# Five edits around the first Mamba block and the last output, and three ways of weighing a Mamba state

## The reference, cut to what matters

```python
u = _silu(cb + sum((xpad[:, k:k + Ls, :] * cw[:, k] for k in range(DCV))))
dt = jax.nn.softplus(jnp.einsum('blr,cr->blc', dt_in, dw) + db)
def step(h, inp):
    dt_t, B_t, C_t, u_t = inp
    dA = jnp.exp(dt_t[..., None] * A)
    h = dA * h + (dt_t * u_t)[..., None] * B_t[:, None, :]
    y = jnp.einsum('bcn,bn->bc', h, C_t)
    return (h, y)
y = (ys + u * Dp) * _silu(z)
m = _layernorm(m + einsum('blc,dc->bld', y, wo), ln_g, ln_b)
```

## Time and profile before

| | us |
|---|---|
| median of 3 runs (2123.95 to 2128.16) | 2124.9 |
| the profiled execution | 2123.37 |
| its span, first to last instruction | 2121.5 |
| PE, DVE, ACT, POOL busy in it | 1841.3, 1634.3, 1323.1, 1015.5 |
| first scan of Mamba starts | 35.4 |
| last operation of the first block on DVE | 815.1 |
| mean granted TensorE clock | 0.943 of 2.4 GHz |

### The profile page before, as it was taken

The page is one execution under the profiler, slowest core; times in us unless marked ns, Lnnn a source line. Parts: engine busy times, 40 slices in busy tenths (PEclk is TensorE's granted clock), DMA queues, the critical chain, the costliest instruction groups (busy, mean ns, idle before and its releaser), DMA issues. The chain is left out here.

```text
span 2121.5 us, 49383 instructions
## 1 busy us (share of the span) xinstructions
PE 1841.3 (87%) x19527; PEld 1346.4 (63%) x19527; DVE 1634.3 (77%) x2595; ACT 1323.1 (62%) x2681; POOL 1015.5 (48%) x782
## 2 busy tenths in 40 slices
PE   8899889898888778987878787897798799999999
PEld 4444444444443335445567787676776599999999
DVE  5999999999999994768475442546544689998996
ACT  6988887778876643123544444342646488888886
POOL 3787777777777881100037777200630133333333
PEclk9999999999999998997879999898988799999999
DMA  5444444444445441600148889303720411112000
GB/s 191 128 137 140 132 145 134 136 140 133 136 140 144 133 115 41 155 9 1 28 127 270 253 264 249 86 0 116 245 65 12 191 66 66 66 66 77 7 7 7
DMA packets 98037, 241.63 MB, mean 114 GB/s; under 512 B 15024, under 2 KB 48320, under 8 KB 95504
## 3 DMA queue, kind: packets, MB, share of 16 engines
q1 hardware_dynamic: 89120, 218.12, 33.4%
q0 software_dynamic: 7680, 15.74, 3.2%
q10 hardware_dynamic: 1008, 4.62, 0.6%
HBM read 226.25 MB, written 12.19 MB: 112 GB/s over the span
## 5 line engine op out<-in xcount | busy, mean ns | idle before, releaser
L1346 POOL TENSOR_TENSOR dBu<-du,Bs 128x858 f32<-128x858 f32 (+1 forms) x240 | 589.2, 2457 | 184.4 <-DVE hst L1251 95.0
L573 PE MATMUL py<-hst,ident 128*128 128x429 f32 (+1 forms) x960 | 405.9, 551 | 78.6 <-DVE hst L1261 78.3
L1251 DVE TENSOR_TENSOR_SCAN hst<-dA,dBu 128x858 f32<-128x858 f32 (+1 forms) x240 | 458.3, 1910 | 6.6 <-ACT dA L1036 4.0
L573 PEld LDWEIGHTS py<-hst,ident 128*128 128x128 f32 x960 | 178.1, 197 | 269.3 <-DVE hst L1261 150.4
L1036 ACT ACTIVATE dA<-dt,negA 128x416 f32<-128x416 f32 (+1 forms) x480 | 269.9, 596 | 115.2 <-DVE hst L1251 113.5
L3671 POOL TENSOR_TENSOR hm<-h,mw 128x264 f32<-128x264 f32 x128 | 89.8, 701 | 390.7 <-DVE h L3651 390.7
L1261 DVE TENSOR_TENSOR hst<-hst,Cs 128x858 f32<-128x858 f32 (+1 forms) x240 | 247.3, 1030 | 0.0
L3542 PE MATMUL pg<-xm,wi 128*128 128x66 f16 x6144 | 214.3, 195 | 8.2 <-issue 6.8
L3542 PE MATMUL pg<-hs,wh 128*128 128x66 f16 x6144 | 217.5, 194 | 2.9 <-issue 2.9
L3542 PEld LDWEIGHTS pg<-xm,wi 128*128 128x128 f16 x6144 | 201.6, 98 | 12.8 <-issue 7.5
L3542 PEld LDWEIGHTS pg<-hs,wh 128*128 128x128 f16 x6144 | 203.8, 98 | 6.5 <-issue 3.1
(11 more groups left out here) (600 smaller groups left out, 3471.5 us busy)
## 6 DMA issues: line engine op xcount, KB each, us to landing
wb<-sf_w SPq DMA_DIRECT2D x96, 514.0 KB, 5.3
Bs<-bc_rows SPq DMA_DIRECT2D x96, 429.0 KB, 4.6
Cs<-bc_rows SPq DMA_DIRECT2D x96, 429.0 KB, 3.5
mw<-route_weights SPq DMA_DIRECT2D x8, 2112.0 KB, 10.0
wb<-gf_w SPq DMA_DIRECT2D x24, 514.0 KB, 4.9
Bs<-bc_rows SPq DMA_DIRECT2D x24, 396.0 KB, 5.2
Cs<-bc_rows SPq DMA_DIRECT2D x24, 396.0 KB, 4.3
mb<-route_masks SPq DMA_DIRECT2D x8, 1088.0 KB, 12.7
```

The source lines that it names most:

```text
L573: return nc.tensor.matmul(out, weight, moving, **kw)
L1251: v.tensor_tensor_scan(hst[:, g % HR, 0:2 * n], dA[:, g % 2, 0:2 * n], dBu[:, g % 2, 0:2 * n], 0.0, ALU.mult, ALU.add).then_inc(h_ready, 1)
L1346: g_.tensor_tensor(dBu[:, g % 2, 0:2 * n].rearrange("p (a n) -> p a n", a=2), du[:, j % 2, :, 0:n], Bs[:, q % NBS, k % BG, 0:n].unsqueeze( ...
```

## The change

- avg and eps are set by DVE memsets instead of transfers; cen is now transferred first, and PE and ACT wait for two transfers and two memsets.
- The first operation of `soften` becomes `soften_high`, and runs earlier for item 0.
- dBu of state 0 is made on DVE; POOL begins with state 1.
- Units 3 and 4 are normalised after k = 8 of item 0, behind soften; root(4) moves from k = 10 to k = 8 of ACT's queue; POOL waits for all five units at k = 10 of item 0.
- Each state gets a kind. S is as before. With D, the scan writes into dA in PSUM, and DVE weighs at once, from PSUM into hst; decay(g+2) then waits for that weighing and first sets the first column of each sequence to zero again by an ACT copy from the tile zero. With P, the scan is as before and POOL weighs, behind dBu(g+2). Item 0 has only S. In items 1 to 11 the states 8, 9, 12, 13 are D and 10, 14 are P. In items 12 to 14 the states 2 to 13 follow D, D, P, D, D, P and so on. That is 138 S, 68 D and 34 P.
- `weighed` is split in two semaphores, `weighed` and `weighed_pool`; SP and PE wait for either.
- `turn_over` before the last products has 15 products instead of 28.

```diff
@@ -373,6 +373,25 @@
 LSTM_ITEMS = S // PER_ITEM
+IN_LSTM = {8: "D", 9: "D", 10: "P", 12: "D", 13: "D", 14: "P"}
+def kind(g):
+    j, k = g // DST, g % DST
+    if j <= LSTM_ITEMS:
+        return IN_LSTM.get(k, "S") if j >= 1 else "S"
+    return "DPD"[k % 3] if 2 <= k < DST - 2 else "S"
+def by_vector(g):
+    return sum(kind(i) != "P" for i in range(g + 1))
+def by_gpsimd(g):
+    return sum(kind(i) == "P" for i in range(g + 1))
@@ -399,6 +418,7 @@
         edge = sb("edge", [128, 6])
+        zero = sb("zero", [128, 2 * SQ])
         u = sb("u", [128, 2, 2, SCW])
...
@@ -560,7 +580,9 @@
                     if q >= NBS:
-                        sp.wait_ge(weighed, BG * (q - NBS + 1))
+                        sp.wait_ge(weighed, by_vector(BG * (q - NBS + 1) - 1))
+                        if by_gpsimd(BG * (q - NBS + 1) - 1):
+                            sp.wait_ge(weighed_pool, by_gpsimd(BG * (q - NBS + 1) - 1))
                     sp.dma_start(Cs[:, q % NBS, :, 0:n], rows(j, DST, k)).then_inc(c_loaded[q % NBS], 16)
@@ -718,7 +740,10 @@
                         mm(py[:, h, 0:n], diag[:, l, h, :], u[:, j % 2, h, 0:n], start=True, stop=False)
-                pe.wait_ge(weighed, g + 1)
+                if kind(g) == "P":
+                    pe.wait_ge(weighed_pool, by_gpsimd(g))
+                else:
+                    pe.wait_ge(weighed, by_vector(g))
                 for h in range(2):
@@ -761,7 +786,8 @@
             tokens(1)
-            pe.wait_ge(const_loaded, 64)
+            pe.wait_ge(const_loaded, 32)
+            pe.wait_ge(consts_set, 2)
             center(0)
@@ -972,6 +998,7 @@
                     low_step(1)
+                    root(4)
@@ -1029,7 +1056,11 @@
                     act.wait_ge(dt_done, j + 1)
-                if g >= 2:
+                if g >= 2 and kind(g - 2) == "D":
+                    act.wait_ge(zero_set, 1)
+                    act.wait_ge(weighed, by_vector(g - 2))
+                    a(by_seq(dA[:, g % 2, 0:2 * SCW])[:, :, 0], zero[:, :], ACT.Copy)
+                elif g >= 2:
                     act.wait_ge(h_ready, g - 1)
@@ -1046,7 +1077,8 @@
             nc.scalar.preload_act_table_set("natural_log_exp_and_others")
-            act.wait_ge(const_loaded, 64)
+            act.wait_ge(const_loaded, 32)
+            act.wait_ge(consts_set, 2)
             first_square()
@@ -1097,8 +1129,8 @@
                         keep_center(3 + k // 7)
-                    if k in (6, 10):
-                        root(3 + k // 10)
+                    if k == 6:
+                        root(3)
                     if k == 9:
@@ -1141,6 +1173,8 @@
             v.memset(blank, 0.0).then_inc(blanked, 1)
+            v.memset(cst["avg"], 1.0 / 128).then_inc(consts_set, 1)
+            v.memset(cst["eps"], EPS).then_inc(consts_set, 1)
             v.memset(xd[DTR + 2 * DST:DTR + 2 * DST + 1, :, :], 1.0).then_inc(ones_set, 1)
@@ -1186,11 +1220,14 @@
-            def soften(j):
+            def soften_high(j):
                 l, at, n = item(j)
...
                 v.tensor_tensor(e[:, :, 0:n], pos[:, :, 0:n], e[:, :, 0:n], ALU.add).then_inc(high_ready, 1)
+            def soften(j):
+                l, at, n = item(j)
                 dve.wait_ge(low_ready, j + 1)
@@ -1244,11 +1281,12 @@
                 l, at, n = item(j)
-                if g >= HR:
+                if g >= HR and kind(g) != "D":
                     dve.wait_ge(y_added, g - HR + 1)
...
                 dve.wait_ge(dA_ready, g + 1)
-                v.tensor_tensor_scan(hst[:, g % HR, 0:2 * n], dA[:, g % 2, 0:2 * n], dBu[:, g % 2, 0:2 * n], 0.0, ALU.mult,
+                o = dA[:, g % 2, 0:2 * n] if kind(g) == "D" else hst[:, g % HR, 0:2 * n]
+                v.tensor_tensor_scan(o, dA[:, g % 2, 0:2 * n], dBu[:, g % 2, 0:2 * n], 0.0, ALU.mult,
                                      ALU.add).then_inc(h_ready, 1)
@@ -1258,7 +1296,12 @@
                 h = hst[:, g % HR, 0:2 * n].rearrange("p (a n) -> p a n", a=2)
-                v.tensor_tensor(h, h, Cs[:, q % NBS, k % BG, 0:n].unsqueeze(1).broadcast_to([128, 2, n]),
+                x = h
+                if kind(g) == "D":
+                    x = dA[:, g % 2, 0:2 * n].rearrange("p (a n) -> p a n", a=2)
+                    if g >= HR:
+                        dve.wait_ge(y_added, g - HR + 1)
+                v.tensor_tensor(h, x, Cs[:, q % NBS, k % BG, 0:n].unsqueeze(1).broadcast_to([128, 2, n]),
                                 ALU.mult).then_inc(weighed, 1)
@@ -1273,19 +1316,27 @@
             first_square_large()
+            soften_high(0)
             copy_gate(1)
...
             soften(0)
+            l, at, n = item(0)
+            dve.wait_ge(du_done, 1)
+            dve.wait_ge(b_loaded[0], 16)
+            v.tensor_tensor(dBu[:, 0, 0:2 * n].rearrange("p (a n) -> p a n", a=2), du[:, 0, :, 0:n],
+                            Bs[:, 0, 0, 0:n].unsqueeze(1).broadcast_to([128, 2, n]), ALU.mult).then_inc(dBu_ready, 1)
             for g in range(NI * DST):
...
                 scan(g)
-                if g >= 1:
+                if g >= 1 and kind(g - 1) == "S":
                     weigh(g - 1)
-                if j == 0 and k in (3, 7, 11):
-                    scale_unit(2 + k // 4)
+                if kind(g) == "D":
+                    weigh(g)
+                if j == 0 and k == 3:
+                    scale_unit(2)
                 if 1 <= j <= LSTM_ITEMS:
@@ -1295,7 +1346,11 @@
                     if j + 1 < NI:
+                        soften_high(j + 1)
                         soften(j + 1)
+                    if j == 0:
+                        scale_unit(3)
+                        scale_unit(4)
                     if j >= 2:
@@ -1319,9 +1374,20 @@
+            def weigh(g):
+                j, k = g // DST, g % DST
+                l, at, n = item(j)
+                q = g // BG
+                pool.wait_ge(h_ready, g + 1)
+                pool.wait_ge(c_loaded[q % NBS], 16 * (q // NBS + 1))
+                h = hst[:, g % HR, 0:2 * n].rearrange("p (a n) -> p a n", a=2)
+                g_.tensor_tensor(h, h, Cs[:, q % NBS, k % BG, 0:n].unsqueeze(1).broadcast_to([128, 2, n]),
+                                 ALU.mult).then_inc(weighed_pool, 1)
             for at, value in enumerate((BELOW_ONE, KAPPA / 2, -KAPPA * KAPPA / 6, LOG_KAPPA, CAP, KAPPA * KAPPA / 12)):
...
             g_.memset(whh[:, :, :, :], 0.0).then_inc(l_zeroed, 1)
+            g_.memset(zero[:, :], 0.0).then_inc(zero_set, 1)
             pool.wait_ge(w0_loaded, 16)
@@ -1337,14 +1403,22 @@
                         pool.wait_ge(du_done, j + 2)
+                    if j == 0:
+                        pool.wait_ge(normed, NSC)
                     if j >= 2:
...
                     pool.wait_ge(b_loaded[q % NBS], 16 * (q // NBS + 1))
-                if g >= 2:
+                if g == 0:
+                    continue
+                if g == 1:
+                    pool.wait_ge(dBu_ready, 1)
+                else:
                     pool.wait_ge(h_ready, g - 1)
...
                                  Bs[:, q % NBS, k % BG, 0:n].unsqueeze(1).broadcast_to([128, 2, n]), ALU.mult).then_inc(dBu_ready, 1)
+                if g >= 2 and kind(g - 2) == "P":
+                    weigh(g - 2)
                 if j in (1, NSC + 1) and k in (2, 4, 6, 8):
@@ -3580,7 +3654,7 @@
             output(TS // GR - 1, 0, GR - 1)
-            turn_over(nc, cst, py[:, 256:384], 28)
+            turn_over(nc, cst, py[:, 256:384], 15)
             output(TS // GR - 1, GR - 1, GR)
@@ -4031,10 +4105,8 @@
     c["ident"] = np.eye(128, dtype=np.float32)
-    c["avg"] = np.full((128, 128), 1.0 / 128, np.float32)
     c["mdct"] = mdct_constant().reshape(128, 256)
-    c["cen"] = np.eye(128, dtype=np.float32) - c["avg"]
-    c["eps"] = np.full((128, 1), EPS, np.float32)
+    c["cen"] = np.eye(128, dtype=np.float32) - np.full((128, 128), 1.0 / 128, np.float32)
     return c
@@ -4044,10 +4116,10 @@
         cst, constants = {}, []
-        for name in ("ident", "avg", "cen", "eps"):
-            t = sbuf(nc, ctx, name, list(a["c_" + name].shape))
-            cst[name] = t[:, :]
-            constants.append((t[:, :], a["c_" + name]))
+        for name, shape in (("cen", [128, 128]), ("ident", [128, 128]), ("avg", [128, 128]), ("eps", [128, 1])):
+            cst[name] = sbuf(nc, ctx, name, shape)[:, :]
+        for name in ("cen", "ident"):
+            constants.append((cst[name], a["c_" + name]))
         cst["x_in"] = [Counted(ctx.enter_context(nc.semaphore(f"x_in{j}"))) for j in range(UN)]
```

8 lines of the change are left out of this document (4 added, 4 removed).

## The result

The changed kernel takes 2160.3 us (median of 4 runs, 2153.5 to 2165.3) against 2125.8 us for the kernel before, measured beside it: a ratio of 1.0156, 95% interval 1.0136 to 1.0175. It is 34 us slower. The profiled execution, the shortest of the four, took 2153.5 us, with a span of 2151.6 and a mean granted TensorE clock of 0.935 of 2.4 GHz; in the slower runs it was 0.928.

The account below looks back on a forecast made before the run. The prediction took DVE to set the pace. Its terms -1.15, +4.1, +35.3, -1.2 and -2.8 made +34 us on the median of 2124.9, stated as 2158, with a range of 2128 to 2172.

Parts of the forecast that it names:

- item 0: Units 3 and 4 and root(4) moved in item 0: later decays delay scans 9, 10 and 12; +4.1 us (0 to +5).
- (a): Scan 8 to scan 10, items 1 to 11: weighing 9 moves ahead of lstm_c; +1.0 us per item on average.
- (c): Scan 12 to scan 2 of the next item: later decays delay xd, PE's second delta and the gate; +1.45 us per item.
- the prices of D and P: DVE time per state: D 2.97 us for scan and weighing, P 1.85; a scan writing PSUM is no slower.
- the end: Fewer turn_over fillers before the last products: last output starts earlier, -2.8 us (bounds -2.9 and -2).
- (b): Scan 10 to scan 12: decay 11 waits for weighing 9, so tanh, table loads and decay 12 come later; +0.87 us per item.
- the opening: Start of the kernel: memsets replace transfers, dt starts earlier; -1.15 us (bounds -0.5 and -2.4), dBu 0 worth nothing at scan 2.
- DVE's busy time: Sign to look for in the changed profile: DVE busy time down by 30 us while Mamba lasts longer.
- items 12 to 14: D D P triples save 2.4 us an item, less shut-out instructions and table loads: +1.2, -0.9, -1.5, sum -1.2 us.
- the one in which only ScalarE's queue counts: Rival: PE catches up before the gate and DVE regains the loss there; total 2137 us, chance 0.18.
- The one with dearer D states and the stall on top of the gate's wait: Rival: D states cost 0.3 us or more extra, or weighing 15's stall adds to the gate; 2173 us, chance 0.10.
- The one in which DVE's sum decides: Rival, faster: 34 weighings leaving DVE save 32 us, D weighings give back 5.6; 2091 us, chance 0.12.

## Why the prediction came out as it did

The time (2158; by the sum of the terms, 34.25 on 2124.9, it should have read 2159) and the sign were right. Of the steps, item 0, (a), (c), the prices of D and P and the end held in size; (b) held in mechanism and was too large; the opening, DVE's busy time and items 12 to 14 didn't hold, each for a reason of its own.

*Opening, -1.15 forecast.* Too small, and hidden in the profile by another thing. Scan 0 starts at 32.21 instead of 35.41, scan 2 at 38.13 instead of 40.33: -2.2. I had bound scan 2 to work of ACT that "doesn't move", and it moved with the rest; scan 4 is still 2.2 us earlier (45.91 instead of 48.11). But scan 5 starts at 50.94, after 50.91 before, with 2.16 us of waiting for ACT's decay, because PE, whose products feed ACT there, ran slowly. Windows of the changed kernel (length, then busy us of PE, PEld, DVE, ACT and POOL, granted clock, DMA share, GB/s):

```profile
36.00:42.00 6.00, 3.93 (x8) 1.75 (x7) 4.99 (x5) 4.31 (x8) 4.36 (x3) 0.77 0.14 50
42.00:48.00 6.00, 6.00 (x12) 2.87 (x12) 5.89 (x5) 3.07 (x6) 3.46 (x3) 0.66 0.97 302
```

In the kernel before both have 1.00. It isn't the change that does it: the kernel before with only the shorter end, whose opening is untouched, has 0.74 there (first line), and the one with 8 D, 9 D, 10 P, whose opening is the changed one, has 1.00 (second):

```profile
36.00:48.00 12.00, 8.76 (x15) 3.96 (x16) 11.70 (x8) 9.59 (x18) 10.88 (x5) 0.74 0.40 110
```

```profile
36.00:48.00 12.00, 9.61 (x27) 4.55 (x26) 10.99 (x9) 10.05 (x20) 7.91 (x4) 1.00 0.53 184
```

The step from scan 4 to scan 5 follows the clock and not the kernel: 2.8 us at 1.00, 3.5 to 3.8 at 0.86, 5.0 to 5.1 at 0.74 and below; the step behind it is 3.4 us at 1.00 and 3.8 below. Together that is 2.7 us by which the profile of the changed kernel is longer and that of the kernel before isn't. With like clocks the gain of the opening stays: item 1 starts at 94.67 in the changed kernel and at 93.04 in the one with only the shorter end, +1.6 and not +4.6, and with 1.00 at 91.92 and 92.46 in two changed kernels against 90.09, +1.8 and +2.4. With +4.1 for item 0 the opening is then worth 1.7 to 2.5 us.

*Item 0, +4.1 forecast.* Right, with its places: scan 9 at 70.66 (forecast 70.1), scan 10 at 76.44 (76.0), scan 12 at 83.47 (83.0), and 4.1 us between two kernels that are alike up to item 12 but for it.

*(a) Scan 8 to scan 10, +1.0.* Right: 10.80 in item 8 instead of 9.71, 7.33 and 3.47; over the eleven items 10.6 us, 0.96 each.

*(b) Scan 10 to scan 12, +0.87.* Right in its mechanism, and the term of the eleven items that was most too large: 6.74 instead of 6.05, so +0.7, and 7.4 us in eleven items instead of 9.6. The tanh starts 0.85 us after scan 10 (forecast 1.0), and the kernel with state 9 as S shows that it is weighing 9 which holds it.

*(c) Scan 12 to scan 2' of the next item, +1.45.* Near in size: +1.25 in item 8, and 13.8 us in eleven items where 14.9 were forecast (ten times 1.45, and 0.4 for item 11). Xd starts 5.14 us after scan 12 (forecast to end near 5.8: it does, at 5.65), the second delta product at 9.06 (9.3), the gate at 18.74 (18.95, before 17.48), all a little earlier than I put them. The mechanism was half of it. I let PE alone make the gate late and booked nothing for a stall of weighing 15. In five of the eleven items the gate waits for PE; in the other six it waits for nothing, since weighing 15 in its stall, or dBu 1' where the weighing came first, makes DVE just as late. The run with state 15 as D shows that PE alone gives nearly the same: item by item it is within 0.25 us of the run with 12, 13 and 14 alone. In item 11, which no LSTM products follow, the forecast was 0.4 and the measured +1.1, with the stall as with 15 as D. That the two limits lie so close was luck, and not something that I had worked out.

Together (a) to (c) cost 31.8 us and not 35.3: 10.6, 7.4 and 13.8.

*DVE's busy time down by 30 us while it lasts.* Wrong: it fell by 12.3. 34 weighings of 1.03 us left it, 35 us, and the 138 that stayed S grew from 1030 to 1146 ns, which gives 16 us back. These 16 us are eleven stalls of about 1.4 us: weighing 15 in nine of the items 1 to 11, and weighing 14 in items 12 and 13. I had named both, the one as hidden in the wait for the gate and the other with 1.4 us, and counted neither as busy time. In items 2 and 7 weighing 15 takes 1.03 us, and dBu 1', which starts within 0.02 us of it, takes 2.75 instead. The two figures make 19 us. Added up one by one DVE's instructions are 22.5 us shorter; the page's busy time counts once where two overlap at their edges, and there are 10 us less of that. In the Trainium skill, SBUF — State Buffer, section Who interferes with whom, a VectorE instruction with two SBUF inputs contends with a GpSimd instruction that reads SBUF, for a lock that only one of them holds, and one with a single SBUF input doesn't contend. By that rule the stalls of 2.46, 2.59 and 2.61 us and the undisturbed D weighings of 1.03 to 1.05 us belong together, and the traces here agree with it on both: D weighing 9 of item 8 (511.91) takes 1.05 us while GpSimd's product runs from 510.15 to 513.81.

*Items 12 to 14, -1.2 forecast.* The wrong sign: +1.3 of their own. (Another 1.4 us stand in item 12 and belong to (c) of item 11.) The failed step is the price of what waits in items 13 and 14. In item 13 I forecast -0.9 and found +0.1: soften gave back 0.8 (forecast 0.4), weighing 14 gave back 1.6 (1.4), the gate and a late dBu another 0.5 that I hadn't booked, and against these the triples saved 2.6 (2.4). In item 14 I forecast -1.5 and found -0.3: I had booked no wait of scans for a decay or for PE, and they made 1.5 us. Item 12 was near: scan 12 stands 9.9 us after scan 9 (forecast 10.1, before 8.7), and the item has +1.6 where I said +1.2.

*D price 2.97, P price 1.85, the scan in PSUM no slower.* 2.95, 1.85, and 1.94 against 1.93 to 1.94.

*The end, -2.8.* -2.6: the fillers shrink as forecast, but the sixteen last products take 1.96 instead of 1.72 us. It isn't the lower clock that I had allowed for: the granted clock there is 1.00 before and after. What it is stays open. In the changed kernel:

```profile
2141.32 3.38 PE py L134 x30
2144.70 0.11 issue
2144.81 1.96 PE py L3646 x16
```

*The sum.* -1.15, +4.1, +35.3 and -1.2 made 37.0 for the first block, and 37.7 were measured. That is closer than the terms deserve. Measured by the same terms it is -2.2, +4.1, +31.8 and +1.3, which is 35.0, and 2.7 of a clock that the kernel doesn't set. The eleven items were 3.5 us too large, items 12 to 14 2.5 us too small, the opening 1.1 us too small a gain, and the clock of one profiled execution closed the gap. The medians, 34.5 us apart, stand on several executions; 35.0 less 2.6 for the end is 32.4, and the ratio gives 33 us with an interval of 29 to 37. So the forecast of +34 was right, with errors in the terms that partly cancelled.

Of the rivals, the one in which only ScalarE's queue counts held for (b) but not for the gate: from scan 12 to scan 2' 13.8 us were lost where it had nothing. The one with dearer D states and the stall on top of the gate's wait fell with a D price of 2.95 and with the run with 15 as D. The one in which DVE's sum decides fell twice: scan 12 shows that ScalarE's queue is next in line, and the runs with P at 6 or 7, where nothing but DVE sets the pace, show that not even there does the sum shrink.

## What to carry to other kernels

Before an output is moved into the buffer of an input, ask which engine refills that buffer and what stands in its queue behind the refill: here the weighing on VectorE cost 0.15 us more, and the tanh, the two table loads and the next decay that came to wait for it 1.3 us, 1.5 with the wait for PE behind them. Work that is handed from VectorE to GpSimd is to be priced with the VectorE instruction that meets it: if both its inputs are in SBUF and GpSimd's instruction is running, it stands for the rest of it, and 1.4 to 1.6 us were paid for the 0.94 saved. An edit that shortens the busiest engine gains up to the place where the next one is late, so look for the shortest wait that another engine ends (0.25 and 0.41 us here) before counting the savings.
